# Attention scores computed in both orders, four row groups at a time, in place of transposed exponentials

## What is computed

```python
x = x + xattn(layernorm(x), ctx, ctx, Wq, bq, Wk, bk, Wv, bv, interference, amp, Wo, bo)
x = x + ffn(layernorm(x), ...)
# xattn, b=32, s=64, H=16, M=4, dk=8:
qh, kh, vh = (proj(q, Wq, bq), proj(k, Wk, bk), proj(v, Wv, bv))       # (b, H, s, dk, M)
qh, kh, vh = (t + 0.1 * amp * einsum('bhsdi,hij->bhsdj', t, interference) for t in (qh, kh, vh))
scores = einsum('bhqdm,bhkdm->bhqkm', qh, kh) / sqrt(dk)
weights = softmax(scores, axis=3)                                      # over the 64 keys
out = einsum('bhqkm,bhkdm->bhqdm', weights, vh) ... @ Wo.T + bo
# ffn:
w = sc[g_idx] * (wq - zq[g_idx])                                       # gate/up 512 x 2752, down 1376 x 512
h = silu(x @ w_gate) * (x @ w_up);  y = h @ w_down
```

## Time and profile before

| | us |
|---|---|
| median of 3 runs | 929.61 (928.64 to 932.58) |
| the profiled execution | 931.81 |
| its span, first to last instruction | 930.1 |
| setup, up to the first scores | 0 to 114.45 |
| chunk 0, from its first scores | 114.45 to about 242 |
| chunks 1 to 7 | about 242 to 879 |
| feed-forward of the last chunk | 879 to 930 |
| issue of the load of Wo (SP) | 7.29 |

### The profile page before, as it was taken

One profiled execution on the slowest core, in us unless ns is written; L12 is line 12 of the kernel. 1 busy time (PEld: TensorE's weight loads), 2 busy tenths in 40 slices (PEclk: granted clock), 3 DMA queues, 4 the chain that ended last, 5 costly groups with the idle time before them and its releaser, 6 DMA issues.

```text
span 930.1 us, 19580 instructions
## 1 busy us (share of the span) xinstructions
PE 802.7 (86%) x7352; PEld 581.1 (62%) x7361; DVE 654.8 (70%) x1436; ACT 496.4 (53%) x902; POOL 310.4 (33%) x289
## 2 busy tenths in 40 slices
PE   5315477886999999999999999999999999999898
PEld 5303333442678667856785778577857786786484
DVE  8987577776569756966797579658965886588521
ACT  1225477776467445745663557266726672666120
POOL 6313744544134213421351144114411542044011
PEclk9657755555999999999999999999999999999899
DMA  8900122321000020002000200110011000100000
GB/s 245 279 23 0 47 62 62 84 68 55 30 18 2 13 82 2 1 23 72 1 1 25 70 1 1 46 49 1 1 47 47 1 2 23 25 2 2 23 1 23
DMA packets 20689, 36.36 MB, mean 39 GB/s; under 512 B 3374, under 2 KB 7602, under 8 KB 20592
## 3 DMA queue, kind: packets, MB, share of 16 engines
q1 hardware_dynamic: 20604, 35.08, 13.0%
HBM read 26.56 MB, written 4.19 MB: 33 GB/s over the span
## 4 chain that ended last, share of the span: by engine, by line
issue 43%; PE 21%; POOL 15%; DVE 13%; ACT 6%; DMA 1%; another core or an unknown queue 1%; POOLq 0%; SPq 0%; ACTq 0%; DVEq 0%
POOL arena L1275 8%; PE bank L499 6%; PE bank L514 4%; POOL arena L1267 4%; PE bank L480 2%; DVE WGU L1010 2%; PE bank L470 2%; POOL arena L1258 2%; DVE arena L1037 1%; PE bank L612 1%; PE bank L434 1%; PE bank L624 1%; ACT arena L758 1%; POOL rstd L1253 1%; PE bank L435 1%
## 5 line engine op out<-in xcount | busy, mean ns | idle before, releaser
L499 PE MATMUL bank<-arena,WGU 128*128 128x256 f16 (+1 forms) x2112 | 262.1, 274 | 1.6 <-DVE arena L690 1.4
L1275 POOL TENSOR_TENSOR arena<-arena,negmax 128x512 f32<-128x512 f32 x128 | 133.4, 1042 | 360.6 <-DVE negmax L1148 360.6
L499 PEld LDWEIGHTS bank<-arena,WGU 128*128 128x128 f16 (+1 forms) x2112 | 204.1, 100 | 29.1 <-DVE arena L690 1.8
L863 ACT ACTIVATE arena<-arena,small 128x512 f32<-128x512 f32 x128 | 92.4, 722 | 84.3 <-POOL arena L1275 84.2
L514 PE MATMUL bank<-WD,arena 128*128 128x512 f16 (+1 forms) x528 | 129.1, 379 | 0.0
L690 DVE SCALAR_TENSOR_TENSOR arena<-bank,arena 128x512 f16<-128x512 f32 x160 | 108.1, 687 | 27.3 <-ACT arena L680 26.1
L470 PE MATMUL bank<-arena,WT 128*128 128x256 f16 x768 | 92.7, 280 | 38.5 <-DVE arena L690 35.3
L680 ACT ACTIVATE arena<-bank 128x512 f16<-128x512 f32 x160 | 92.7, 594 | 45.7 <-PE bank L624 32.6
L470 PEld LDWEIGHTS bank<-arena,WT 128*128 128x128 f16 x768 | 76.3, 101 | 55.4 <-issue 42.9
L1148 DVE TENSOR_REDUCE negmax<-arena 128x8 f32<-128x512 f32 x128 | 87.3, 682 | 31.1 <-ACT arena L850 30.1
L624 PE MATMUL bank<-ident,arena 128*128 128x128 f32 x512 | 87.2, 297 | 21.3 <-ACT arena L863 16.3
(11 more groups left out here) (145 smaller groups left out, 1030.4 us busy)
## 6 DMA issues: line engine op xcount, KB each, us to landing
arena<-in_L_ffn_qweight_gu SPq DMA_DIRECT2D x8, 688.0 KB, 5.2
arena<-arena SPq DMA_DIRECT2D x32, 132.0 KB, 2.4
WT<-in_ctx SPq DMA_DIRECT2D x8, 512.0 KB, 14.8
arena<-in_ctx SPq DMA_DIRECT2D x8, 512.0 KB, 3.4
arena<-in_x SPq DMA_DIRECT2D x8, 512.0 KB, 3.7
out_y<-arena SPq DMA_DIRECT2D x16, 256.0 KB, 2.1
arena<-in_L_ffn_qweight_down SPq DMA_DIRECT2D x10, 256.0 KB, 3.4
arena<-in_L_xattn_Wk SPq DMA_DIRECT2D x1, 1024.0 KB, 7.0
```

Of the source, the lines that this page charges most:

```text
L499: mm = e.matmul(pb[0:m, i * TOK:(i + 1) * TOK], WGU[:, sp, kb, half * INTER + fb * P:half * INTER + fb * P + m], x2T[:, mp, kb, :], start= ...
L863: e.activation(pring[:, step % 2, :], pring[:, step % 2, :], ACT.Exp, scale=KSM).then_inc(S["exp_done"], 1)
L1275: e.tensor_tensor(ring, ring, ap(negmax, 0, P, 8 * (s % 2), [(1, 8), (0, 64)]), ALU.add).then_inc(S["sub_done"], 1)
```

## The change

A chunk's attention is now cut into four batches of four slots instead of eight pairs. For a batch:
- `pe_scores` issues the 48 matmuls of all four slots on four row groups into four banks (AB[0] to AB[3], the former SB and TB).
- DVE takes the four negated maxima straight from PSUM (`dve_max`), adds LIFT (the logarithm of P_SCALE in the units of the scores) and splits the sum into three bf16 parts (`dve_split_max`, four small instructions). PE transposes them with one matmul (`pe_turn_max`), DVE copies the result out (`dve_copy_max`).
- `pe_scores_turned` computes the scores a second time with K and Q exchanged, so that keys lie on partitions: 48 matmuls, and 16 more (4 for each of the four column groups) that add the negated maximum with a selection matrix `sel`, in the same PSUM accumulation.
- ACT takes the exponential from PSUM into pring (four slots deep, `act_exp`), ACT and POOL write hi and lo into phl (also four deep; `act_p_hi`, `pool_p_lo`).
- The values of a batch are computed in the slices of the next batch, the last batch's in the chunk's tail.

Gone are ACT's copy of the scores, POOL's subtraction, PE's transposes of P, and their low halves on DVE. K is projected into AB[0], AB[1] and V into AB[2], AB[3]; only Q uses JB. The transposed tiles of x2 go to GB and UB, the others to AB. The slices are fewer and larger (EACH, TAIL). In the setup `dve_zeros` moves behind the low halves of xT of chunk 0, and the second `pool_hot` directly behind the first. The dequantization units of chunk 0 (ticks) are spread over 28 slots. `dynamic_dma_scratch_size=2048` is new.

```diff
-EXTRA = {8: "cT0", 10: "cT1", 12: "xT0", 14: "xT1", 15: "oT0"}
+EXTRAS = (("cT0",), ("cT1",), ("xT0",), ("xT1", "oT0"))
...
-EACH = (FFN_UNITS - sum(PRE) - sum(POST)) / (2 * STEPS)
+PRE, EACH, TAIL = (24, 44), (14, 12, 10, 10, 11, 11), (16, 12, 12, 16)
...
+TICKS = ND + 3
+FIRST_SLOT = 2
+TICK_ENDS = [0] * FIRST_SLOT + [TICKS * (k + 1) // (SLICES - FIRST_SLOT) for k in range(SLICES - FIRST_SLOT)]
...
-        SB, TB, JB, GB, UB = bank[0:2], bank[2:4], bank[4:6], bank[6], bank[7]
+        AB, JB, GB, UB = bank[0:4], bank[4:6], bank[6], bank[7]
...
+            return {"x2T0": GB, "x2T1": UB, "oT0": AB[2], "oT1": AB[0]}.get(name, AB[1])
...
+            for b in range(NB):
+                slot = IN_BATCH[b]
+                pe_scores(e, c, b)
+                ffn_slice(slot[0])
+                if b:
+                    pe_values(e, c, 4 * b - 4)
+                ffn_slice(slot[1])
+                if b:
+                    pe_values(e, c, 4 * b - 3)
+                ffn_slice(slot[2])
+                pe_turn_max(e, c, b)
+                names = pe_extras(e, c, b)
+                ffn_slice(slot[3])
+                if names:
+                    e.wait_ge(S["t_lo"], t_at(c, names[-1]))
+                pe_scores_turned(e, c, b)
+                ffn_slice(slot[4])
+                if b:
+                    pe_values(e, c, 4 * b - 2)
+                ffn_slice(slot[5])
+                if b:
+                    pe_values(e, c, 4 * b - 1)
...
+        def pe_scores(e, c, b):
+            if b == 0:
+                e.wait_ge(S["qm_ready"], 4 * c + 4)
+                e.wait_ge(S["v_evicted"], 2 * c + 2)
+            else:
+                e.wait_ge(S["exp_done"], SLOTS * c + 4 * b)
...
+        def pe_turn_max(e, c, b):
+            e.wait_ge(S["nm_split"], NB * c + b + 1)
+            e.matmul(AB[0][:, 0:P], nm16[:, :, :, :].rearrange("p a k n -> p (a k n)"), ident16[:, :],
+                     start=True, stop=True).then_inc(S["nm_turned"], 1)
+
+        def pe_scores_turned(e, c, b):
+            e.wait_ge(S["nm_ready"], NB * c + b + 1)
             for i in range(KB):
-                mm = e.transpose(tb[:, i * P:(i + 1) * P], pring[:, s % 2, i * P:(i + 1) * P], ident[:, :])
+                for n, (qp, kp) in enumerate(PASSES):
+                    for a in range(4):
+                        rows = slice(32 * a, 32 * a + 32)
+                        e.matmul(AB[a][:, i * P:(i + 1) * P],
+                                 km[rows, kp, NB * i + b, :, :].rearrange("p v t -> p (v t)"),
+                                 qm[rows, qp, NB * i + b, :, :].rearrange("p v t -> p (v t)"),
+                                 start=(n == 0), stop=False)
+                for a in range(4):
+                    rows = slice(32 * a, 32 * a + 32)
+                    mm = e.matmul(AB[a][:, i * P:(i + 1) * P], sel[rows, i, :], nmT[rows, :], start=False, stop=True)
...
+        def act_exp(e, c, s):
+            a = s % 4
+            e.wait_ge(S["st_done"], SLOTS * c + s + 1)
+            reached(e, S["p_lo"], SLOTS * c + s - 3)
+            e.activation(pring[:, a, :], AB[a][:, :], ACT.Exp, scale=KSM).then_inc(S["exp_done"], 1)
...
+                act_slot(e, c, slot[3], first)
+                act_exp(e, c, 4 * b)
+                act_exp(e, c, 4 * b + 1)
+                act_slot(e, c, slot[4], first)
+                act_exp(e, c, 4 * b + 2)
+                act_exp(e, c, 4 * b + 3)
+                act_p_hi(e, c, 4 * b)
+                act_slot(e, c, slot[5], first)
+                for a in range(1, 4):
+                    act_p_hi(e, c, 4 * b + a)
...
+                dve_max(e, c, 4 * b), dve_max(e, c, 4 * b + 1)
+                dve_slot(e, c, slot[0], first)
+                dve_max(e, c, 4 * b + 2), dve_max(e, c, 4 * b + 3)
+                dve_split_max(e, c, b)
+                if b:
+                    dve_o(e, c, 4 * b - 4)
+                dve_slot(e, c, slot[1], first)
+                if b:
+                    dve_o(e, c, 4 * b - 3)
+                dve_slot(e, c, slot[2], first)
+                dve_copy_max(e, c, b)
+                for name in EXTRAS[b]:
+                    if name in (T_LAST if last else T_ORDER):
+                        dve_lo(e, c, name)
```

More of the change, by code:

```diff
@@ new lines, in dve_chunk @@
+            dve_slot(e, c, 1, first)
+            for b in range(NB):
+                slot = IN_BATCH[b]
+                dve_max(e, c, 4 * b), dve_max(e, c, 4 * b + 1)
[9 more added lines that the diff above has]
+                dve_copy_max(e, c, b)
+                for name in EXTRAS[b]:
+                    if name in (T_LAST if last else T_ORDER):
+                        dve_lo(e, c, name)
+                dve_slot(e, c, slot[3], first)
+                if b == 0 and not last:
+                    dve_stats_next(e, c)
+                if b == 1 and not last:
+                    dve_apply_next(e, c, first)
+                dve_slot(e, c, slot[4], first)
+                if b:
+                    dve_o(e, c, 4 * b - 2)
+                dve_slot(e, c, slot[5], first)
+                if b:
+                    dve_o(e, c, 4 * b - 1)
@@ L1162, in dve_chunk @@
+            dve_slot(e, c, AT_TAIL[0], first)
+            dve_o(e, c, SLOTS - 4)
+            dve_slot(e, c, AT_TAIL[1], first)
+            for k in range(SLOTS - 3, SLOTS):
+                dve_o(e, c, k)
+            dve_slot(e, c, AT_TAIL[2], first)
             dve_lo(e, c, "oT1")
[L1163 to L1165 removed]
+            dve_slot(e, c, AT_TAIL[3], first)
+            if first:
+                e.memset(T4, 0.0).then_inc(S["y_ready"], 2)
```

346 lines of the change are left out of this document (165 added, 181 removed).

## The result

The kernel after the change takes 937.06 us (median of 6 runs, 936.29 to 938.67), the kernel before 929.62 beside it (6 runs, 928.64 to 932.58): ratio 1.0076, 95% interval 1.0059 to 1.0093. It is slower, by 7.4 us and not by the 35 forecast. The profiled execution has a span of 936.9 us against 930.1, +6.8. First the two stretches that answer to the earlier trace rows: busy us and instructions by engine, PEclk, DMA.

A forecast was written before the change was run, and what follows sets the result against it. PE was taken to bound the middle chunks, DVE the setup, and a PE, ACT, DVE, PE chain chunk 0. Sum: 931.8 + 34 + 3 - 2 = 966.8, predicted as 965 us; range 920 to 986.

The forecast's parts named there:

- The price of a score matmul: Attention on PE: 448 score matmuls a chunk on four row groups at 28 ns each, 12.5 us, +6.3 a chunk.
- The lower bound: Score matmuls of a chunk: 7.2 us, if four row groups run beside each other as two do now.
- The estimate of 17 ns: Score matmul price from the Trainium skill: 7.8 us a chunk, which would lower the kernel's sum by 33 us.
- The new waits: PE waiting in a middle chunk for DVE's maxima chain, the exponentials and the last low halves: 8.3 us a chunk.
- rival 4: POOL's low halves of P hold DVE's small split instructions: +2 to +3 us a chunk, 983; 0.20 together with Rival 5.
- the list of signs: Expected in the changed trace, among others: L1163 to L1169 at 0.2 us each, or 1 us by rival 4.
- What goes: Middle chunk: 16 transpose groups (7.4 us), PE's idle ahead of them (2.1) and at the chunk's start (0.8): -10.3 us.
- Middle chunks: Seven later chunks: -10.3 + 6.3 + 0.5 + 8.3 = +4.8 us each, times 7 = +34 us.
- Chunk 0: First chunk, with dequantization: +3 us, and +12 more if four row groups go no faster than two.
- Rival 5: Chunk 0 is lengthened by serial blocks: +12 us, 977; chance 0.20 together with rival 4.
- Setup: Zero points leave DVE's chain, but the Wo copies wait for POOL instructions and end near 41: -2 us.
- Rival 1: Four row groups run truly beside each other, 7.2 instead of 12.5 us a chunk: -37 us, 928; chance 0.15.

The follow-up runs named there:

- e2: The changed kernel with the negated maxima and the rest of their split kept in PSUM instead of SBUF: 920.86 us, ratio 0.989 to the kernel before.
- e7: The changed kernel with the split of the maxima placed behind the dequantization's product on DVE, in chunk 0 alone: 930.93 us, ratio 1.0013 to the kernel before.

## Why the prediction was wrong in size and right in sign

- **The price of a score matmul** is the step that failed: "28 ns, nearer to that row". 28 instead of 16 ns, 448 times in seven chunks, is 5.3 x 7 = 37 us, more than the whole miss of 28. Two errors made it. The 0.77 us of 24 matmuls was read as 32 ns each, one behind the other. They are 12 rounds of 56 ns, with one matmul of each of the two groups in a round, and 0.11 us of the block's own; with four groups a round is as long and holds four. "Nothing shows pairs coming faster" than 31 ns was not so even in the trace of before: 16 score matmuls start in 0.42 us there, two by two. And the bound by L640 was taken from matmuls of 66 columns and 128 rows, all four row groups at once, which say nothing of four small ones side by side. The lower bound, half of what two groups take, was the right value, and its argument (time scales with the clock, thus array time) stood in the text. The estimate of 17 ns from the Trainium skill (TensorE: Matmul & The Clock Gate, "Measured speedup vs the span model") came close to the 16 measured over a block of 48. The floor of about 25 ns from start to start on the same page doesn't hold between groups: within a round the starts are 2 to 5 ns apart.
- **The new waits** were right in place and kind: L644 for L714 and L712, L624 for the exponential. Together 10.0 us where 8.3 stood (and the first four of that sum, 2.3 + 1.6 + 1.2 + 0.5, make 5.6, not the 5.8 written). The turned scores cost 5.1, the turning matmul 3.0 where 0.3 stood for the third batch. The missing part is rival 4's, the split held by POOL: e2 takes it away and gains 16 us. In each of the second to fourth batch of the middle chunk one or two of L1163 to L1169 took 0.6 to 1.1 us; the list of signs had 1 us.
- **What goes**, 10.3 us, holds with the sum above to 0.3 us.
- **Middle chunks**: +34 forecast, +6.4 measured: -37 for the matmuls, +12 for the waits (1.7 x 7), -2 left over.
- **Chunk 0**: +3 forecast, +9.3 measured. Rival 5's mechanism (serial blocks) is real: e7 moves one of them and 5.7 us go.
- **Setup**: -2 forecast, -9.0 measured. Rightly held by POOL, but only two of the 16 copies for a whole POOL instruction, so they ended at 33.73 and not near 41.

Rival 1 came true in its price, rival 4 in its mechanism, part of 5 in its size. The bounds, taken together, held the time; the chosen value inside them did not. The sign was partly luck: with the right price and all else as forecast the sum is rival 1's 928, level with before. That the kernel came out slower is owed to the waits (+12) and chunk 0 (+6), both too small in the forecast, less the setup (-7). The share of 0.15 for rival 1 was too small for a case whose only evidence against was a row of other work.

## What to carry to other kernels

Before you put a price on one of many small matmuls, look at the starts of single ones: cut the timeline a fraction of a microsecond behind a block's first start and count. If the row groups start together, the price is that of one row group's matmul divided by the groups used, plus the block's own part. The mean over a block (32, 26 or 16 ns here) carries over to no other number of groups. A chain within one stage, PE to DVE to PE, is as long as what stands ahead of its links in DVE's order: put the link that PE waits for first (here 22 us by moving two small outputs), and keep its operands in PSUM while GpSimd works (16 us). When a gain of PE's work leaves the time unchanged, list PE's waits of one period before and after, and add them up.
